# Four graph layers in one program per engine, with row statistics in two portions, on Trainium2

## The reference

```python
x = _layernorm(x + _L0_gnn_ref(x, adj, L0_gnn_W, L0_gnn_a), axis=-1)
x = _layernorm(x + _L1_gnn_ref(x, adj, L1_gnn_W, L1_gnn_a), axis=-1)   # 1 head, the same, then ELU
x = _layernorm(x + _L2_gnn_ref(x, nodemask, adj, ...), axis=-1)        # gated sum over neighbours, relu
x = _layernorm(x + _L3_gnn_ref(x, adj, L3_gnn_Wq, ...), axis=-1)       # 4 heads of dot-product attention, projection
```

## Time and profile before

| | us |
|---|---|
| median of 3 runs | 851.84 (847.98 to 851.87) |
| the profiled execution, its own time | 851.46 |
| its span, first to last instruction | 845.6 |
| mean granted clock of TensorE | 0.956 of full speed |
| PE busy | 708.5 (84%) |
| VectorE busy | 618.2 (73%) |
| ScalarE busy | 563.5 (67%) |
| GpSimd busy | 399.7 (47%) |

### The profile page before, as it was taken

One profiled execution on the slowest core, in us unless ns is written; L12 is line 12 of the kernel. 1 busy time (PEld: TensorE's weight loads), 2 busy tenths in 40 slices (PEclk: granted clock), 3 DMA queues, 4 the chain that ended last, 5 costly groups with the idle time before them and its releaser, 6 DMA issues. The chain is left out here.

```text
span 845.6 us, 26213 instructions
## 1 busy us (share of the span) xinstructions
PE 708.5 (84%) x8450; PEld 521.7 (62%) x8482; DVE 618.2 (73%) x1758; ACT 563.5 (67%) x1266; POOL 399.7 (47%) x615
## 2 busy tenths in 40 slices
PE   5589999999998467877872899995999999999992
PEld 3456666666665345655651799983666666667661
DVE  4168778778787537888887488885677777877865
ACT  1346666666665368888882899974777787777771
POOL 0447777878777313433432111112545555455540
PEclk9999999999998959999997799997999999999996
DMA  1523333333321022222220333321222222222211
GB/s 46 143 49 93 95 94 76 80 92 93 93 57 40 1 31 26 27 31 32 25 31 0 88 86 83 84 60 19 33 58 43 51 55 56 45 54 50 58 45 38
DMA packets 34919, 47.76 MB, mean 56 GB/s; under 512 B 4394, under 2 KB 18484, under 8 KB 34868
## 3 DMA queue, kind: packets, MB, share of 16 engines
q0 software_dynamic: 18576, 21.01, 15.6%
q1 hardware_dynamic: 16292, 26.10, 9.8%
HBM read 51.33 MB, written 8.39 MB: 71 GB/s over the span
## 5 line engine op out<-in xcount | busy, mean ns | idle before, releaser
L490 DVE SCALAR_TENSOR_TENSOR pp<-banks,floor,adj 128x1024 f32<-128x1024 f32 x128 | 157.3, 1249 | 2.9 <-PE banks L585 2.5
L1110 POOL TENSOR_TENSOR pp<-pp,adj 128x512 f32<-128x512 f32 x64 | 73.5, 1166 | 119.0 <-ACT pp L1151 119.0
L416 ACT COPY rows<-banks 128x640 bf16<-128x640 bf16 x64 | 44.3, 692 | 70.5 <-PE banks L562 70.3
L585 PE MATMUL banks<-pp,yv 128*17 128x128 f32 x2048 | 82.9, 281 | 1.5 <-DVE pp L490 1.4
L716 POOL TENSOR_TENSOR yres<-oo,x 128x512 f32 (+1 forms) x32 | 40.7, 1273 | 91.6 <-DVE oo L818 91.6
L1151 ACT ACTIVATE pp<-banks,nobound 128x512 f32<-128x512 f32 x128 | 81.5, 696 | 2.9 <-PE banks L1333 1.3
L572 PE MATMUL banks<-rows 32*128 32x128 bf16 x1024 | 51.8, 221 | 21.4 <-DVE pp L490 19.7
L1029 PE MATMUL banks<-w2b,xt 128*128 128x256 f32 x256 | 62.4, 388 | 0.0
L340 POOL TENSOR_TENSOR yv<-wh,yv 128x512 f32<-128x512 f32 x32 | 35.2, 1099 | 52.3 <-ACT yv L409 52.3
L913 POOL DMA_DIRECT2D adj<-in_adj x32 | 17.0, 533 | 86.1 <-ACT sq L948 75.1
L421 ACT COPY ot<-banks 128x512 f32<-128x512 f32 x64 | 37.4, 584 | 28.4 <-PE banks L585 28.4
(11 more groups left out here) (219 smaller groups left out, 1953.6 us busy)
## 6 DMA issues: line engine op xcount, KB each, us to landing
adj<-in_adjt POOLq DMA_DIRECT2D x96, 128.0 KB, 3.0
xt<-in_xt SPq DMA_DIRECT2D x32, 256.0 KB, 3.7
x<-in_x SPq DMA_DIRECT2D x32, 256.0 KB, 3.2
adj<-in_adj POOLq DMA_DIRECT2D x32, 256.0 KB, 3.0
out_ngd<-yres SPq DMA_DIRECT2D x32, 256.0 KB
w3q<-in_wq SPq DMA_DIRECT2D x1, 64.0 KB, 1.9
w3k<-in_wk SPq DMA_DIRECT2D x1, 64.0 KB, 1.8
ident<-in_ident SPq DMA_DIRECT2D x1, 64.0 KB
```

The costliest lines, as they stand in the source:

```text
L416: nc.scalar.copy(rows[:, slot % 2, a, :], R[:, 0:5 * N]).then_inc(s["rw"], 1)
L490: nc.vector.scalar_tensor_tensor(pp[:, g], S[g % 2][:, :].rearrange("p (h n) -> p h n", n=N), floor[:, slot:slot + 1], adj[:, slot, g:g + ...
L585: ins = nc.tensor.matmul(O[32 * h:32 * h + w, c:c + N], yv[:, slot % 2, g * H + 4 * half + h, :], pp[:, g, 4 * half + h, :], start=True, s ...
L1110: nc.gpsimd.tensor_tensor(pp[:, slot % 2, h], pp[:, slot % 2, h], adj[:, slot], ALU.mult).then_inc(s["pm"], 1)
```

## The change

The four layers and the verdict are no longer phases of their own. Each layer function returns its engines' programs (`Programs`), and one new phase, `layers`, makes a single block in which each engine runs the programs of layers 0 to 3 and of the verdict one after the other, without a barrier. The SBUF tensors of all layers are placed by hand (`Plan`) in one area of 104 KB, in which neighbouring layers share only places whose content is done with by the order of the waits.

`row_statistics` gives way to `Rows`, in three parts: `variance` (VectorE), `roots` (ScalarE, with Ln and Exp in place of Sqrt) and `refine` (VectorE, one Newton step in place of the reciprocal). Each is done in two portions, the first 120 columns and the last 8, and they stand within the ends and the beginnings of the layers' programs. Some last pieces of a layer (`tail` on GpSimd, `last` on VectorE) run after the first pieces of the next layer. In `single` the order on ScalarE and TensorE is new. The request for the table set moves from `heads` to the beginning of ScalarE's program in `multi`.

The diff, cut to its core and shown without changes of indentation:

```diff
+class Rows:
...
+    def variance(self, dve, portion):
...
+        dve.wait_ge(self.link, 8 * portion + 5)
+        nc.vector.tensor_tensor(v, v, d, ALU.add).then_inc(self.var, 1)
+
+    def roots(self, act, portion):
+
+        nc, c = self.nc, self.columns(portion)
+        act.wait_ge(self.var, portion + 1)
+        nc.scalar.activation(self.rstd[:, c], self.v[:, c], ACT.Ln).then_inc(self.log, 1)
+        act.wait_ge(self.log, portion + 1)
+        nc.scalar.activation(self.rstd[:, c], self.rstd[:, c], ACT.Exp, scale=-0.5).then_inc(self.root, 1)
+
+    def refine(self, dve, portion):
+
+        nc, c = self.nc, self.columns(portion)
+        r, d, v = self.rstd[:, c], self.d[:, c], self.v[:, c]
+        dve.wait_ge(self.root, portion + 1)
+        nc.vector.scalar_tensor_tensor(d, r, -0.5, r, ALU.mult, ALU.mult).then_inc(self.link, 1)
+        dve.wait_ge(self.link, 8 * portion + 6)
+        nc.vector.tensor_tensor(d, d, v, ALU.mult).then_inc(self.link, 1)
+        dve.wait_ge(self.link, 8 * portion + 7)
+        nc.vector.scalar_tensor_tensor(r, d, 1.5, r, ALU.add, ALU.mult).then_inc(self.link, 1)
+        dve.wait_ge(self.link, 8 * portion + 8)
+        nc.vector.scalar_tensor_tensor(self.nmr[:, c], self.mean[:, c], -1.0, r, ALU.mult, ALU.mult).then_inc(self.done, 1)
...
@@ multi, ScalarE
+        nc.scalar.preload_act_table_set("natural_log_exp_and_others")
             for n in range(3):
...
             evac_turned(T - 1, (T - 1) % RING, 0)
+        after.roots(act, 0)
             evac_turned(T - 1, (T - 1) % RING, 1)
@@ multi, VectorE
             steps(dve, step, end)
+        dve.wait_ge(s["stats"], T - 2)
+        after.variance(dve, 0)
             statistics(T - 2, (T - 2) % RING)
+        after.refine(dve, 0)
             invert(T - 1, (T - 1) % RING)
             statistics(T - 1, (T - 1) % RING)
+        dve.wait_ge(s["stats"], T)
+        after.variance(dve, 1)
@@ single, GpSimd
+        pool.wait_ge(layer0.projected, 2 * T)
             for n in range(3):
                 load_adj(n, n)
+        layer0.tail()
@@ single, ScalarE
                 need(act, s["xt_tr"], n + 1)
-                need(act, s["we"], n - 1)
+            need(act, s["ab"], n - 1)
                 nc.scalar.copy(xt[:, slot % 2, :], XT[:, :]).then_inc(s["xt"], 1)
...
             normalize(0, 0)
-            evac_xt(0, 0)
             normalize(1, 1)
-            row_exp(0, 0)
+        evac_xt(0, 0)
             column_exp(0, 0)
+        row_exp(0, 0)
+        before.roots(act, 1)
             evac_xt(1, 1)
             normalize(2, 2)
-            normalize(3, 3)
-            row_exp(1, 1)
             column_exp(1, 1)
-            evac_xt(2, 2)
+        row_exp(1, 1)
+        normalize(3, 3)
 
             def step(t, slot, lap):
+            if not known(t) or t + 2 < T:
+                evac_xt(t + 2, (slot + 2) % R8)
                 if not known(t) or t >= 1:
                     elu(t - 1, (slot - 1) % R8)
-                if not known(t) or t + 2 < T:
-                    row_exp(t + 2, (slot + 2) % R8)
+            if not known(t) or t + 4 < T:
+                normalize(t + 4, (slot + 4) % R8, 0, 2)
                 if not known(t) or t + 2 < T:
...
                 if not known(t) or t + 4 < T:
-                    normalize(t + 4, (slot + 4) % R8)
-                if not known(t) or t + 3 < T:
-                    evac_xt(t + 3, (slot + 3) % R8)
+                normalize(t + 4, (slot + 4) % R8, 2, NG)
+            if not known(t) or t + 2 < T:
+                row_exp(t + 2, (slot + 2) % R8)
 
             steps(act, step, end, R8)
             elu(T - 1, (T - 1) % R8)
+        after.roots(act, 0)
@@ single, VectorE
             weights(0, 0, 0)
+        before.refine(dve, 1)
...
+        dve.wait_ge(s["stats"], T - 2)
+        after.variance(dve, 0)
             elu(T - 1, (T - 1) % R8)
             statistics(T - 2, (T - 2) % R8)
+        after.refine(dve, 0)
+
+        def last():
             statistics(T - 1, (T - 1) % R8)
+            dve.wait_ge(s["stats"], T)
+            after.variance(dve, 1)
@@ single, TensorE, expand
                 need(pe, s["xt"], n + 1)
-                need(pe, s["p"], n - 1)
-                nc.tensor.matmul(AB[slot % 2][:, :], k["wa1rep"][:, :], xt[:, slot % 2, :], start=True, stop=True).then_inc(s["ab"], 1)
                 need(pe, s["y"], n)
...
                 ins.then_inc(s["we"], 1)
+            need(pe, s["p"], n - 1)
+            nc.tensor.matmul(AB[slot % 2][:, :], k["wa1rep"][:, :], xt[:, slot % 2, :], start=True, stop=True).then_inc(s["ab"], 1)
@@ relational
             load_adj(1, 1)
+        layer1.tail()
...
             evac_xt(1, 1)
+        before.roots(act, 1)
             tanh(0, 0)
...
             steps(act, step, 26, R8)
+        after.roots(act, 0)
...
-            for n in range(3):
-                normalize(n, n)
+        normalize(0, 0)
+        layer1.last()
+        normalize(1, 1)
+        normalize(2, 2)
             values(0, 0)
+        before.refine(dve, 1)
 
             def step(t, slot, lap):
+            if known(t) and t == T - 1:
+                dve.wait_ge(s["stats"], T - 2)
+                after.variance(dve, 0)
...
+        after.refine(dve, 0)
@@ heads
-            nc.scalar.preload_act_table_set("natural_log_exp_and_others")
             nc.scalar.activation(rise[:, :], k["excess"][:, :], ACT.Exp).then_inc(s["rise"], 1)
...
             evac_v(0, 0)
+        before.roots(act, 1)
             act.wait_ge(s["set"], 1)
...
             normalize(0, 0)
+        layer2.last()
             normalize(1, 1)
...
             queries(0, 0)
+        pe.wait_ge(layer2.finished, T)
             keys(0, 0)
@@ build
-        phase(multi, pb, k, yres, stats, rall, c["x"], c["xt"], c["adjt"])
-        phase(row_statistics, 0, stats, mean, rstd, nmr)
...
-        phase(heads, pb, k, yres, stats, mean, rstd, rsum, c["adjt"], out_ngd)
-        phase(verdict, pb, k, rec1, adjbad, rsum, rall, flag)
+        phase(layers, fast, pb, k, c, yres, stats, rall, rec1, adjbad, rsum, flag, out_ngd)
```

More of the change, by code:

```diff
@@ L46, in known, with sync, gpsimd, scalar @@
     return isinstance(t, int)
+class Programs:
+    def sync(self, f):
+        self.sp = f
+    def gpsimd(self, f):
+        self.pool = f
+    def scalar(self, f):
+        self.act = f
+    def vector(self, f):
+        self.dve = f
+    def tensor(self, f):
+        self.pe = f
+class Plan:
+    def __init__(self, nc, base, runs):
+        self.nc, self.runs = nc, [[base + a, base + b] for a, b in runs]
+    def __call__(self, name, shape, dt):
+        size = math.prod(shape[1:]) * (2 if dt == BF16 else 4)
+        size = (size + 31) // 32 * 32
+        run = next(r for r in self.runs if r[1] - r[0] >= size)
+        run[0] += size
+        return self.nc.alloc_sbuf_tensor_at(name, shape, dt, offset=run[0] - size)
@@ L272, in multi @@
     end = 26
[L274 to L367, removed]
-                in2 = not known(t) or t + 2 < T
-                if in2:
-                    load_adj(t + 2, a2)
-                    high(t + 2, a2)
-                if not known(t) or t + 1 < T:
-                    values(t + 1, a1)
-                if in2:
-                    low(t + 2, a2)
-                if not known(t) or t >= 1:
-                    divide(t - 1, c0)
-                    residual(t - 1, c0, lap - (1 if slot == 0 else 0))
-            steps(pool, step, end)
@@ L689, in single @@
+    return block
+def single(nc, sb, sem, pb, k, yres, stats, before, after, rec, layer0, adjt):
     w, R8 = D + 1, 8
@@ L734, in normalize, with _ @@
+    @block.scalar
+    def _(act):
+        def normalize(n, slot, first=0, last=NG):
+            if first == 0:
+                if known(n):
+                    act.wait_ge(before.done, 1 if n < T - 2 else 2)
                 need(act, s["y_out"], n - 5)
-                for g in range(NG):
-                    at = n * NG + g
-                    ins = nc.scalar.activation(xr[:, slot, g, :], flat(at), ACT.Identity, bias=nmr[:, bass.ds(at, 1)], scale=rstd[:, bass.ds(at, 1)])
+            for g in range(first, last):
+                at = n * NG + g
+                ins = nc.scalar.activation(xr[:, slot, g, :], flat(at), ACT.Identity, bias=before.nmr[:, bass.ds(at, 1)], scale=before.rstd[:, bass.ds(at, 1)])
+            if last == NG:
@@ new lines, in _, with step @@
+        transpose_x(0, 0)
+        queries(0, 0)
+        pe.wait_ge(layer2.finished, T)
+        keys(0, 0)
+        transpose_x(1, 1)
+        vals(0, 0)
+        pe.wait_ge(s["set"], 1)
+        def step(t, slot, lap):
+            a1, a2, c0 = (slot + 1) % RING, (slot + 2) % RING, (slot - 1) % RING
+            in1 = not known(t) or t + 1 < T
+            in2 = not known(t) or t + 2 < T
+            inc = not known(t) or t >= 1
+            scores(t, slot)
+            if in2:
+                transpose_x(t + 2, a2)
+            if in1:
+                keys(t + 1, a1)
+            if inc:
```

(9 more changed lines are left out.)

1752 lines of the change are left out of this document (931 added, 821 removed).

## The result

The changed kernel takes 944.73 us (938.64 to 947.48, four runs), the kernel before 850.84 beside it (847.98 to 851.87): ratio 1.110, 95% interval 1.104 to 1.116. It is slower. The forecast was 922, the range 908 to 950. The profiled execution took 947.48, with a span of 942.6 and 4.9 around it, against 851.46, 845.6 and 5.9 before.

A forecast was written before the change was run, and what follows sets the result against it. Each layer had its own bound: TensorE the head layer (7.60 us a step), waits the one-head layer (4.46, VectorE needing 3.67). Sum: 851.5 - 0.5 - 9 - 22 - 6 + 112 - 0.5 - 3.3 = 922.2 us, range 908 to 950.

The forecast's parts named there:

- Terms 1 and 2: Start of layer 0: table load moved to the front, -0.5 us; seam of layers 0 and 1: earlier normalization, -9 us.
- Term 3: Layer 1: new order on ScalarE and TensorE cuts the step from 4.46 to 3.72 us, -22 us.
- Rival (b): Loads come, but layer 1 keeps 4.46 us because TensorE hands the extended product over late: 944 us, chance 0.12.
- Term 4: Seam of layers 1 and 2: first normalization starts near 459 instead of 465.16, -6 us.
- Term 6: Seam of layers 2 and 3: table loads at the roots take back most of the earlier start, -0.5 us.
- rival (a): After Tanh the compiler takes the combined set by itself, so the head layer's loads don't come: 808 us, chance 0.15.
- Term 5: Head layer: request lost at Tanh, four table loads in a step with roots, 11.28 instead of 7.60 us, +112 us.
- rival (c): Head layer: TensorE's clock falls to the lower level in its pauses, query copies wait: 965 us, chance 0.07.
- (d): Head layer: switching sets costs ScalarE as much again as the load, step near 16.8 us: 1083 us, chance 0.02.
- Term 7: End of the kernel: verdict starts at once, with the output transfer beside it, -3.3 us.

## Why the prediction was right, and where it was short

By its terms, against the profiled execution (947.5 measured, 922.2 forecast, 25.3 apart).

**Terms 1 and 2.** Forecast -0.5 and -9, together -9.5; measured -11.3 at the first aggregation. The chain came as written: the statistics of group 29 start 0.65 earlier (285.83 against 286.48), refinement ends at 290.92 against a forecast 291.3, normalization starts 9.7 earlier. Short was the part behind it. From normalization to aggregation are 11.4 us instead of 13.0. The difference is more than the 1.3 of the load, so that the two normalizations ahead of the first evacuation, for which I had taken something off, seem to cost nothing; no run separates the two.

**Term 3.** Forecast 3.72 a step and -22; measured 3.72 and 138.1 - 115.3 = -22.8, and the old order put back confirms it by +24. Rival (b), layer 1 keeps 4.46, is out.

**Term 4.** Forecast -6: from the last aggregation to the first Tanh were 472.93 - 451.80 = 21.1 and are 433.00 - 417.65 = 15.35, that is -5.8. **Term 6.** Forecast -0.5; from Tanh to the first exponentials are 114.6 against 114.4: +0.2. The loads at this seam cost some 2.5 us, for with one line more the exponentials start at 545.1 and not at 547.6; without them the term would be -2.3, near the -2.5 that rival (a) had for it. With terms 1 to 4 the exponentials start 39.7 earlier where 38 was forecast.

**Term 5**, the term that turned the sign, was right in its loads and short in its size: forecast +112, measured 389.0 - 249.8 = +139.3. That each Ln and the Exp behind it would cost a load each, and not share the combined set, was my estimate. No run shows how the compiler chooses a set; the groups of the changed kernel show four loads in each step (L1262, L1265, L1271 and L1273, x32 each, 1283 ns). The parts now have sizes. The loads themselves: at most +112.9 between first and last exponentials (keys made thrice), against 110.4 + 2.4 forecast. The clock: +23.4 or a little more, the changed kernel's 372.9 less 349.5. The rest, 3.0, is at the end and was not taken apart: from the last exponentials to the last result are 16.2 us instead of 13.2, where I counted 1.3 for the last root's loads and took 2.1 off for copies.

So the step that failed is the sentence that "TensorE, VectorE and GpSimd do in 11.28 what they do in 7.60 and are covered". They have the time, but TensorE no longer has the clock: it pauses 1.4 us before the keys and 1.8 before the projection, and behind the second pause it may run at the lower level (0.50 from 590 to 593). This was rival (c), with a price of 1.4 a step, which is what most late copies show (0.6 to 1.8, and 2.35 the last). Not every step has it: of the 13 query copies between 567 and 716, nine are late and four are on time, a mean of 0.94 over all 32, and so the rival's 43 us became 23. Its chance of 0.07 was too low. I had argued that no pause is like the 12 us of the earlier trace rows; but those 12 us, 0.50 from 296 to 300, only show what a pause so long does, and no row that I had read shows pauses of 2 us with the clock that follows them. By the bounds of its own terms, 908 to 932, the forecast would have missed the time; the range held it because it went up to 950 for (b) and a part of (c). That 944.7 is also the 944 of (b), which is out, is chance. And the sign set for (d), a step of 16.8, is not its own sum: 11.28 + 4 x 1.3 = 16.5.

**Term 7.** Forecast -3.3; from the end of the last result to the end of the span are 5.9 us instead of 8.5, -2.6. Around the span are 4.9 instead of 5.9, which I had left as it was.

**Rivals (a) and (d).** (a), the combined set is chosen by itself, is out by the 135 loads; the time it gave, 808, is what the kernel takes when the request is made behind Tanh, 805.8. (d), a switch costs as much again, is out by the step of 11.3. That the request at the front is lost is shown in effect: a load stands at L1027, ahead of Tanh, and 132 more behind it, where the same request behind Tanh leaves one, its own (L1053). The runs show where a load stands and not which set it brings.

## What to carry to other kernels

Here the request for an activation table set held only until the first function that made another load, the Tanh: when layers are merged or a prologue is moved, walk ScalarE's whole program, put the request behind the last function that needs another set, and count the table loads in the profile; here that one line was worth 139 us and the rest of the change 45. Here the longer step on ScalarE gave TensorE pauses of 1.4 and 1.8 us and a clock of 0.91 (600 to 700 us), so "it is covered now" must be held, for TensorE, against the granted clock and not only against busy time.

## What the runs showed of the hardware

**Short pauses can cost the clock.** With pauses of 1.4 and 1.8 us in a step of 11.4 TensorE ran at the lower level, granted clock 0.50, after the second pause in nine of 13 steps between 567 and 716 us (projection up to 2.08 instead of 1.16, mean from 600 to 700 us 0.91), and in others with about the same pauses at 1.00; what decides between these steps is not shown. With more products, and without the second pause, it stayed at 1.00 from 545 to 800 us, and the kernel was 21 us faster.

**A load costs its own time.** A load is 1283 ns long. In 128 loads among alternating functions the activation, where its input is there, starts 0.01 to 0.02 us behind the load and nothing else is lost: at full clock a step with four of them is 11.3 us, as the sum of its rows has it. The 128 loads of the head layer take 164.2 us and lengthen it by 112.9, or a little less, at full clock; the 51.3 that are hidden are 1.6 a step, which agrees with the waits that ScalarE had there, 0.26 + 1.30.

**VectorE's mask operation lasted as long as the GpSimd product beside it.** In the changed kernel `nota` on VectorE (mean 1236 ns, 283 before) and the mask's product on GpSimd (mean 1173) start together:

```profile
712.18 1.27 DVE L1324 TENSOR_SCALAR nota<-adj 128x512 bf16<-128x512 bf16 x1
...
712.15 2.32 POOL L1214 TENSOR_TENSOR pp<-pp,adj 128x512 f32<-128x512 f32 x2 [8.64 <-ACT pp L1255]
```

GpSimd starts first, at 712.15, its two products take 2.32 together, and VectorE's operation, 0.28 us long in the kernel before, ends only at 713.45, shortly behind the first, which by the mean ends at 713.32. In the kernel before VectorE started first, and GpSimd at 709.34:

```profile
709.24 0.28 DVE L1214 TENSOR_SCALAR nota<-adj 128x512 bf16<-128x512 bf16 x1
```

With GpSimd's products cut to one column, 0.18 us, it takes 0.30, though GpSimd again starts first. So in these three kernels the length follows GpSimd's product where that starts first; by what mechanism, they do not show. Nor does its row show a wait (idle time 0.0): only its length beside that of the other kernel does.
